# Two transformer layers in one kernel: the write and store of x1 moved one step later in layer 2, the opening transfers and splits of layer 1 moved to other engines

## What is computed

```
x = x1 = layernorm(x + attention1(x))            # multi-LoRA q, k, v, o; rotary embedding; causal softmax
h  = rmsnorm(x1) * ln2_w                         # and rmsnorm(x1) * ln1_w feeds attention2
mod = 0.1 * tanh(attention2(x1) @ A)
gate = silu(h @ W_in.T + mod * (h @ A) @ B)
out = layernorm(x1 + (x1 + gate * (h @ W_up.T) @ W_down.T))
```

## Time and profile before

| | us |
|---|---|
| three runs | 2775.04, 2783.93, 2787.33 |
| median | 2783.93 |
| the profiled execution | 2788.6, of which the span from first to last instruction is 2786.8 |
| PE busy | 2629.9 (94% of the span) |
| DVE busy | 1600.0 (57%) |
| ACT busy | 1325.7 (48%) |
| POOL busy | 667.9 (24%) |
| mean granted PE clock | 0.980 |

### The profile page before, as it was taken

One profiled execution on the slowest core, in us unless ns is written; L12 is line 12 of the kernel. 1 busy time (PEld: TensorE's weight loads), 2 busy tenths in 40 slices (PEclk: granted clock), 3 DMA queues, 4 the chain that ended last, 5 costly groups with the idle time before them and its releaser, 6 DMA issues.

```text
span 2786.8 us, 40960 instructions
## 1 busy us (share of the span) xinstructions
PE 2629.9 (94%) x13584; PEld 2019.6 (72%) x13584; DVE 1600.0 (57%) x4341; ACT 1325.7 (48%) x2739; POOL 667.9 (24%) x535
## 2 busy tenths in 40 slices
PE   6999999999888999999999889999999999999998
PEld 5777777777566666666666647888888888888886
DVE  5777777777847788787787774222222423333333
ACT  3777777777734666666666674111111321111111
POOL 4556555556321322222222221000000000000000
PEclk9999999999889999999999979999999999999999
DMA  6565556665545664565554534111111311111100
GB/s 148 113 146 138 138 124 142 147 144 130 148 120 125 133 131 106 132 132 102 127 132 103 125 83 161 47 47 47 47 47 47 115 47 47 47 47 47 47 30 30
DMA packets 174634, 276.44 MB, mean 99 GB/s; under 512 B 29556, under 2 KB 53876, under 8 KB 173940
## 3 DMA queue, kind: packets, MB, share of 16 engines
q1 hardware_dynamic: 170884, 259.98, 39.1%
q0 software_dynamic: 2304, 12.58, 1.3%
q10 hardware_dynamic: 1264, 1.64, 0.2%
HBM read 97.03 MB, written 42.99 MB: 50 GB/s over the span
## 4 chain that ended last, share of the span: by engine, by line
PE 54%; DVE 9%; issue 3%; ACT 2%; DMA 2%; SPq 1%; POOL 0%; ACTq 0%; DVEq 0%; POOLq 0%
PE lin_ps L2575 13%; PE b_scores_ps L2586 13%; PE b_pv_ps L2556 6%; PE b_scores_t_ps L2556 6%; PE lin_ps L2104 5%; PE b_pv_ps L311 2%; DVE b_prob L294 2%; DVE b_junk L206 2%; PE b_scores_t_ps L275 2%; PE lin_ps L2067 2%; PE b_scores_ps L192 1%; DMA b_k_stack<-b_k_split 1%; PE lin_ps L2581 1%; PE b_scores_ps L2049 1%; SPq L262 1%
## 5 line engine op out<-in xcount | busy, mean ns | idle before, releaser
L286 ACT ACTIVATE b_prob<-b_scores_t_ps 128x384 fp32r<-128x384 f32 (+1 forms) x384 | 201.1, 524 | 218.1 <-PE b_scores_t_ps L277 198.9
L294 DVE TENSOR_TENSOR a_prob<-a_scores_t_ps,a_prob 128x384 fp32r<-128x384 f32 (+1 forms) x384 | 225.3, 593 | 135.7 <-ACT a_scores_t_ps L287 134.2
L294 DVE TENSOR_TENSOR b_prob<-b_scores_t_ps,b_prob 128x384 fp32r<-128x384 f32 (+1 forms) x384 | 225.8, 592 | 100.1 <-ACT b_scores_t_ps L287 100.0
L286 ACT ACTIVATE a_prob<-a_scores_t_ps 128x384 fp32r<-128x384 f32 (+1 forms) x384 | 201.7, 525 | 156.4 <-PE a_scores_t_ps L277 130.8
L311 PE MATMUL b_pv_ps<-b_prob,b_value 128*33 128x512 f32 (+3 forms) x1024 | 273.6, 336 | 0.1
L311 PE MATMUL a_pv_ps<-a_prob,a_value 128*65 128x512 f32 (+3 forms) x1024 | 271.1, 333 | 0.4 <-DVE a_prob L294 0.2
L206 DVE CUSTOM_DVE_ANT_0 b_junk<-b_scores_ps,spare 128x512 bf16<-128x512 f32 (+3 forms) x512 | 226.8, 483 | 66.3 <-PE b_scores_ps L192 63.8
L206 DVE CUSTOM_DVE_ANT_0 a_junk<-a_scores_ps,spare 128x512 bf16<-128x512 f32 (+3 forms) x512 | 226.6, 483 | 26.9 <-PE a_scores_ps L192 24.8
L2519 DVE TENSOR_TENSOR res<-b_scores_ps,b_first_gate 128x512 f32<-128x512 f32 x64 | 44.3, 692 | 331.9 <-PE b_scores_ps L2586 331.9
L2519 DVE TENSOR_TENSOR stage<-b_scores_ps,b_junk 128x512 f32<-128x512 f32 x64 | 44.3, 692 | 328.2 <-PE b_scores_ps L2586 328.2
L1143 PE MATMUL lin_ps<-x_split,w_split 128*128 128x512 f32 x768 | 216.7, 397 | 1.5 <-DVE w_split L938 1.2
(11 more groups left out here) (318 smaller groups left out, 5908.8 us busy)
## 6 DMA issues: line engine op xcount, KB each, us to landing
a_q_stack<-a_q_split SPq DMA_DIRECT2D x192, 128.0 KB, 3.4
a_k_stack<-a_k_split SPq DMA_DIRECT2D x192, 128.0 KB, 3.5
b_q_stack<-b_q_split SPq DMA_DIRECT2D x192, 128.0 KB, 3.1
b_k_stack<-b_k_split SPq DMA_DIRECT2D x192, 128.0 KB, 3.7
spare<-h_t SPq DMA_DIRECT2D x16, 1024.0 KB, 6.2
stage<-in_x_t SPq DMA_DIRECT2D x8, 1024.0 KB, 6.5
a_sum_hi<-a_pv_raw SPq DMA_DIRECT2D x32, 256.0 KB, 3.8
a_inverse_all<-softmax_sums SPq DMA_DIRECT2D x32, 256.0 KB, 3.5
```

The source lines that it names most:

```text
L286: act.activation(at.prob_hi[:, k % at.ring, 0:w], at.scores_t_ps[:, k % 2, 0:w], ACT.Exp, scale=SCALE)
L294: dve.tensor_tensor(at.prob_lo[:, k % at.ring, 0:w], at.scores_t_ps[:, k % 2, 0:w], at.prob_hi[:, k % at.ring, 0:w], ALU.subtract).then_in ...
```

## The change

In layer 2, DVE writes the four tiles of x1 in step 3, slots 6 to 9, each at the end of its slot, and no longer in step 2, slots 8 to 11. SP stores x1 at the end of step 3, behind the stacks of pair 1, and no longer behind the gather at that step's head. The store of batch 0, ahead of the loop, stays. In layer 1's opening SP issues the transfers of `b_stack` and `low_stack`, behind all weight loads; DVE makes the low part of the value weights, behind the constants; ACT rounds the value weights before it copies the first projections out.

```diff
@@ layer 1, SP: opening
                 if n == 1:
                     constants()
+            sp.wait_ge(rows_zeroed, 2)
+            send_b(0)
+            send_low(0)
             for pair in range(2):
                 stack_send(sp, at, 0, 0, pair)
@@ layer 1, POOL
-            pool.wait_ge(w_ready, 2 * KC)
-            for c in range(KC):
-                pool.wait_ge(w_hi, 2 * KC + c + 1)
-                pool.tensor_tensor(w_split[2][:, 1, c, :], w_stage[2][c], w_split[2][:, 0, c, :],
-                                   ALU.subtract).then_inc(w_ready, 1)
@@ layer 1, ACT
-            act.wait_ge(rows_zeroed, 2)
-            act.wait_ge(ab_ready, 2)
...
             weights(0)
             low(0)
-            weights(1)
-            act.wait_ge(low_ready, 1)
...
+            for n in range(1, 3):
+                weights(n)
             for i in range(2):
                 projected(0, 0, i)
-            weights(2)
@@ layer 1, DVE
             constants()
+            weights(2)
@@ layer 2, SP: step(b, g)
                 if not first:
                     gather(*group(b, g, -1))
-                if g == 3 and not last:
-                    store_x1(b + 1)
...
                 if not (last and g >= 2):
                     stack_send(sp, at, *group(b, g, 2), 1)
+                if g == 3 and not last:
+                    store_x1(b + 1)
@@ layer 2, DVE: step(b, g)
                     if g == 2 and not last:
-                        if slot >= UNITS - TT:
-                            normalise_tile(b + 1, slot - (UNITS - TT))
...
                     if slot > 0:
                         for to in left_b(b, g, slot - 1):
                             projected(*to)
+                    if g == 3 and 6 <= slot < 6 + TT and not last:
+                        normalise_tile(b + 1, slot - 6)
```

More of the change, by code:

```diff
@@ L699, in _ @@
             pool.memset(at.value[:, :, :, 2 * HD:2 * HD + 1].bitcast(F32), 1.0).then_inc(at.ones_set, 1)
+            pool.wait_ge(const_in, 80)
             def rope(b, g, i):
@@ L755, in step @@
                         rope(*tile)
-            pool.wait_ge(w_ready, 2 * KC)
-            for c in range(KC):
-                pool.wait_ge(w_hi, 2 * KC + c + 1)
-                pool.tensor_tensor(w_split[2][:, 1, c, :], w_stage[2][c], w_split[2][:, 0, c, :],
-                                   ALU.subtract).then_inc(w_ready, 1)
-            pool.wait_ge(const_in, 80)
             for i in range(2):
@@ L878, in _ @@
             adapter(0)
-            act.wait_ge(rows_zeroed, 2)
-            act.wait_ge(ab_ready, 2)
-            for r, part in enumerate((0, 1, 0)):
-                act.dma_start(b_stack[RANK * r:RANK * (r + 1), :, :].bitcast(F32),
-                              b_split[:, part, :].bitcast(F32)).then_inc(b_stacked, 16)
             weights(0)
             low(0)
-            weights(1)
-            act.wait_ge(low_ready, 1)
-            for r, part in enumerate((0, 0, 1)):
-                act.dma_start(low_stack[RANK * r:RANK * (r + 1), :, :].bitcast(F32),
-                              low_split[:, part, :].bitcast(F32)).then_inc(low_stacked, 16)
+            for n in range(1, 3):
+                weights(n)
             for i in range(2):
                 projected(0, 0, i)
-            weights(2)
             for i in range(2):
```

## The result

| | before | after |
|---|---|---|
| median of 15 runs each, us | 2782.66 | 2791.54 |
| lowest and highest | 2775.04, 2787.52 | 2785.93, 2796.47 |
| ratio, with its 95% interval | | 1.0029 [1.0021, 1.0038] |
| the profiled execution; its span | 2788.6; 2786.8 | 2790.02; 2788.2 |
| PE busy | 2629.9 | 2633.4 |

The change costs 0.29%, that is 8.1 us [5.8, 10.6]. The forecast was + 6.8 us, 2791, a change under 0.5%. The two profiled executions lie only 1.4 us apart, since that of before was at the slow end of its runs; so what follows goes by places, not by the two spans.

What follows compares the result with a forecast made beforehand. PE, busy 2629.9 of 2786.8 us, and its short waits set the end. Terms - 2.6 + 3.0 + 10.8 - 2.0 - 2.4 = + 6.8 on 2783.9 gave 2791 us; 8-in-10 range 2774 to 2802.

Steps and rivals of the forecast that it cites:

- Step 0 behind the store: Layer 2, batches 1 to 6: the store holds the gather 2.6 us; PE loses 1.8 us a batch, 10.8 in all.
- Step 2 without the tiles: Layer 2, end of step 2: k split starts 0.37 us earlier, PE gains that in 7 batches, 2.6 us.
- the other waits of up to 2.4 us come from the queue: Layer 2, k stack waits: argument against gaining all 8.4 us, in the all-gain rival (2769, chance 0.07).
- Step 3 with the tiles: Layer 2, batches 0 to 5: first tile takes up to 1.2 us beside POOL; PE loses 0.5 a batch, 3.0 us.
- The last batch: Its step 0: the k stack's wait goes, the store holding the gather takes part back; a gain of 2.0 us.
- The opening: Layer 1: rotary products run without POOL's split beside them; PE's 2.40 us wait goes, a gain of 2.4 us.

Runs made afterwards that it cites:

- e3: Kernel before with only the store of x1 moved to the end of step 3, the tiles staying in step 2: + 12.5 us [8.9, 16.1].
- e1: Layer 1's opening as in the kernel after, layer 2 as in the kernel before: - 2.8 us [- 5.3, 0.0], 2782.07 beside 2783.52.
- e6: Kernel before, but SP issues the opening transfers of b stack and low stack; POOL still splits the value weights: + 1.4 us [- 1.7, 4.5].
- e7: Kernel before, but DVE, not POOL, splits the value weights in the opening; the transfers stay with ACT: + 0.3 us [- 3.1, 3.6].
- e2: Layer 2 as in the kernel after, layer 1's opening as in the kernel before: + 8.9 us [5.6, 12.2], 2791.61 beside 2783.52.
- e11: Kernel after, but tiles of x1 in slots 8 to 11 of step 3 and POOL storing x1 in its own queue: 2776.29 us beside before's 2782.75, - 6.7.
- e12: As e11, but tiles of x1 in slots 7 to 10 of step 3: 2778.58 us beside before's 2786.20, - 9.8 [- 14.2, - 5.3].
- e5: As e2, but the store cut in two 0.5 MB halves, one at the end of step 3, one behind step 0's gather: + 0.3 us [- 2.2, 2.8].
- e10: As e2, but each store of x1 made twice, so 2 MB stand ahead of step 0's gather: + 29.3 us [24.8, 33.5].
- e4: Kernel before with its old opening, tiles as in the kernel after, store behind the gather of step 0: - 0.8 us [- 3.6, 1.9].

## Why the prediction was right, and where not

The forecast, its range and its sign held, and so did the mechanism that decides. Three of the terms in layer 2 were mis-sized, with opposite signs; that the sum came out this close is in part luck.

- **Step 0 behind the store, + 10.8.** Right in kind, in place nearly. The gather was to be held for 2.6 us. From the start of the step to the release of ACT's copy it was 10.6 us before and 13.4 after in the mean of six batches, 2.8 later. PE lost 1.9 us a batch against the kernel with the store behind the gather (25.88 and 23.98), 1.8 expected: 11.4 us. Against before it is 2.4 a batch, 14.3 us, of which 9.2 lie in slot 6, where the wait is, and 4.5 in slot 7; and the batches differ by more than the 0.3 that I gave, from 1.5 (batch 3) to 2.8 (batch 2) in these two slots. The wait stands at L275 at the end of slot 6, since the transposed scores have but two buffers, and not at L229. The store alone costs 12.5 [8.9, 16.1].
- **Step 2 without the tiles, - 2.6.** Mis-sized. The k split comes 0.45 us earlier, not 0.37, which makes 3.2 us in 7 batches; but the sum of the waits falls by 7.2, near the bound of 8.4, and slots 1 to 3 of step 3, where the waits lie, take 9.8 us less in the seven batches (37.4 for 47.2). The rest of the waits are the long ones of batches 2, 4 and 6, which I had put down to the queue: the stack lands 0.9 to 1.7 us later there than in batches 1, 3 and 5 in before, 0.7 to 1.4 later in e3, and in none of the kernels with the tiles moved. So "the other waits of up to 2.4 us come from the queue", which held this term at 2.6, was no reason to count them out: they went with the tiles. What the 9.8 have beyond the waits is the granted clock (below). In the five profiles with the tiles in step 2 these slots take 43.4 to 47.2 us, in the nine with the tiles moved 37.2 to 37.6.
- **Step 3 with the tiles, + 3.0.** Right in kind, too small: in batches 0 to 5 the first tile takes 0.98 to 1.92 us beside POOL and not up to 1.2, PE's idle time in slot 7 grows by up to 0.95 us a batch, 2.7 in all, and slots 7 and 8 together are 5.5 us longer, above the bound of 4.8. Over all the profiles, slots 7 and 8 take 43.6 to 45.0 us in the seven batches with the tiles in slots 6 to 9 and 39.5 in all the others, those with the tiles in slots 8 to 11 too: the cost is 4.1 to 5.5 us. By the Trainium skill (SBUF — State Buffer, "SBUF: two separate sides") DVE and POOL take their shared ports for a whole instruction. The trace agrees: the tile takes 0.54 us when POOL rests and up to 1.38 more beside its chunks of 1.26 us each, in the longest case (batch 2) a little more than one chunk.
- **The last batch, - 2.0.** Its steps 0 and 1 last 53.4 us in before and 52.1 in after. But in the three other kernels with the old layer 2 (e1, e6, e7) they last 56.6 to 57.2, and in e2 and e3 52.7 and 50.7. In before PE waits 1.77 us for the k stack there at full clock; in those three it waits 2.23 to 2.72, each followed by a granted clock of 0.50; with the store behind the k stack that wait is gone. So it may be 4 us, at the bound, and the profile of before a lucky one. It is not shown: the same two steps take 48.6 us in e11 and 56.0 in e12, which differ by one slot of the tiles.
- **The opening, - 2.4.** In time - 2.8 [- 5.3, 0.0]; in the traces PE's scores start 5 us earlier. I had left out two things: PE goes on 1.0 us sooner with the low stack (25.51 for 26.50), and the granted clock (below).

The sum for layer 2 was + 9.2, and timed it is + 8.9 [5.6, 12.2]. By the steps' lengths in the two profiled executions it is + 6.9 us: step 0 of batches 1 to 6 + 14.3, step 3 - 4.5 (9.8 less in slots 1 to 3, 5.5 more in slots 7 and 8, 0.2 less behind them), steps 1 and 2 - 1.5, the last batch - 1.4. So errors of opposite signs met: the gain of the k stack was taken 7.2 us too small, the losses in step 0 and step 3 up to 3.5 and 2.5 too small. By the Trainium skill (DMA: Bandwidth & Descriptors, "Queues, rings and completion order") descriptors are consumed in ring order. The dose of e5, e2 and e10 agrees: what stands behind the store waits for it in proportion, some 2.5 us a MB.

**What stays open**: why the k stack lands late in batches 2, 4 and 6. The loop runs over two batches at a time, and the transfers of just these stretches hold one packet from an instruction queue, absent in batches 1, 3 and 5. From the transfers by queue in before, at the end of step 2 of batch 4:

```profile
q8 instruction: 1, 0.02, 0.7%
```

But the same packet is there in e2 too, where no stack is late. The 0.45 us by which the stack is issued earlier seem to decide; no run tells how.

## What to carry to other kernels

A large store that nobody waits for is not free where it stands in an in-order queue: ask what is issued next behind it, and who waits for that. Here 1 MB behind the gather cost nothing that can be told, ahead of it 10 us, and ahead of the last stacks, in another queue, as little. And where a batch's pattern of waits alternates, the odd ones may hang on less than the timeline of one batch shows, so look at more than one before sizing a term.

## What the hardware showed that I had not expected

**A wait of PE can be followed by a slow clock, and need not be.** In the opening of before, PE's idle 2.40 us are followed by value matmuls at 2.79 us and then 1.93 for twelve, where 1.60 is the rule; the windows show the granted clock at 0.60 and 0.55. That is 1.5 us on top of the wait, and the new opening gains them too: its four twelves all take 1.60.

```profile
41.04 1.93 PE L1166 MATMUL lin_ps<-w_split,x_split 128*128 128x256 f32 x12
...
44.48 1.60 PE L1166 MATMUL lin_ps<-w_split,x_split 128*128 128x256 f32 x12
```

```profile
38.00:40.00 2.00, 1.75 (x9) 1.78 (x10) 1.64 (x5) 0.59 (x2) 0.87 (x1) 0.60 0.54 112
40.00:42.00 2.00, 2.00 (x12) 2.00 (x12) 0.00 (x0) 0.00 (x0) 1.92 (x3) 0.55 0.75 153
```

In e2, with the same opening, the idle time is 2.76 us and the first two twelves take 2.90 and 2.76; in e4, again the same, it is 1.59 us and they take 1.67 and 1.60:

```profile
37.39 2.90 PE L1166 MATMUL lin_ps<-w_split,x_split 128*128 128x256 f32 x12 [2.76 <-ACT a_rope_in L827]
40.30 2.76 PE L1166 MATMUL lin_ps<-w_split,x_split 128*128 128x256 f32 x12
```

```profile
38.31 1.67 PE L1166 MATMUL lin_ps<-w_split,x_split 128*128 128x256 f32 x12 [1.59 <-ACT a_rope_in L827]
```

So the same 48 value matmuls take 9.1 us in e2 and 6.4 in e4, where the granted clock stays at 1.00, and the waits of 2.40 and 2.76 us cost more than their length.

In layer 2 it is the same, and it is a part of what the change gains. In before, the waits for the k stack of batch 4 (2.40 us) and batch 6 (1.84) are followed by a granted clock of 0.50 for some 3 us:

```profile
1351.32 0.50 PE L192 MATMUL b_scores_ps<-b_k_stack,b_q_stack 112*128 112x512 f32 x1 [2.40 <-DMA b_k_stack<-b_k_split]
```

```profile
1353.00:1354.00 1.00, 1.00 (x5) 0.81 (x3) 0.03 (x1) 0.00 (x0) 0.00 (x0) 0.50 0.17 37
```

In e3, with the tiles still in step 2, none of these waits is, not even one of 2.02 us. Slots 1 to 3 of step 3 are 9.8 us longer in before than in after, of which 7.1 are waits, and 6.0 longer in e3, all of it waits. So the two spells cost some 1.4 us each; e1, with two of them, has 2.8 us beyond its waits, e6 and e7, with one each, 1.5 and 1.6. The length of the wait alone doesn't tell: at L275 of step 0 in batch 2 one of 1.89 us in e3 is followed by 0.50, one of 1.94 in e2 is not.

**SP is slowed too.** Behind the store, two of SP's three issues of the gather take 1.46 and 1.52 us instead of 0.60, so it seems that a full queue is also seen on the engine that feeds it.
